# Window attention in steps of both images at once: scores and transposes share four PSUM banks

## The chip, the cores and the metric

The kernel runs on one core of one Trainium2 chip. The metric is the device time of one execution in microseconds, the median of the runs. A core has the engines TensorE (PE, matrix products and transposes), VectorE (DVE), ScalarE (ACT) and GpSimd (POOL), and SyncE (SP), which issues most DMAs. PE writes only to PSUM, eight banks of 512 float32 in each of 128 partitions; here DVE and ACT read PSUM.

## The reference, cut to what matters

The input is 16 images of 56 x 56 positions and 192 channels. Two residual layers follow each other, each behind a group norm:

```python
x = x + outlook(_gn(x), ...)          # 3 x 3 outlook attention, 6 heads
x = x + window_attention(_gn(x), ...) # 7 x 7 windows, shifted by 3, 12 heads of 16
# window_attention, per window of n = 49 positions:
attn = einsum('wmqd,wmkd->wmqk', q * hd ** (-0.5), k) + rpb + mask
attn = softmax(attn, axis=-1)
out = einsum('wmqk,wmkd->wqmd', attn, v)   # then a projection
```

## The kernel before, in words

Two images are worked on at once. Their 2 x 192 channels are laid on 3 x 128 partitions (tiles j = 0, 1, 2; tile 1 holds the end of the first image's channels and the start of the second's). A hardware loop runs over the 8 pairs of images. In an iteration comes first the outlook layer in seven chunks of eight image rows (replication products of line 481, DVE products, adds on POOL and by DMA), then the window attention in NW = 8 rows of windows.

A row holds 8 windows, that is PAIRS = 4 pairs of windows (p = 0 to 3), for two images. Before, the unit of work is a step s = 0 to 7 of a row: the pair p = s // 2 of one image m = s % 2. A step goes this way: `scores` (PE, 12 products of 32 rows x 64 columns, banks 0 to 3; the profile counts each float32 product twice), `score_bias` (DVE adds the bias to them and writes `sp_`, lines 1540 and 1543), `score_max` (DVE, 1550), `shift_step` (POOL subtracts the maximum, 1777), `exp_step` (ACT, 1127), `prob_sum` (DVE, 1557 and the reciprocal, 1560), `normalize_step` (POOL, 1784), `turn_probs` (PE, six transposes, 737, into banks 6 and 7), `keep_probs` (ACT copies them to `pt`, 1137), and for each two steps `attend` (PE, 24 products of probabilities and values into bank 7, 754) and `keep_y` (DVE, 1565). The scores run AHEAD = 3 steps ahead of the transposes. `sp_` has SOFTS = 4 buffers, `pt` has 3.

The order is written out by hand. Each engine has its own list, and semaphores that only count up join them. Into each step of PE a further piece is put by `ring(w, s)`: the projections of queries and keys of row w + 1 (`wide` makes two of the three output tiles, with two products of 64 rows and then two full ones, lines 336 to 339; `middle` makes the third, with one full product and two of 64 columns, 344 to 346), its values (`window_values`, 682 to 686), the output projection of row w - 1, transposes of the output of row w - 2 (`turn_out`, 772) and transposes of the next pair's input (`turn_next`, 375). Their results go through banks 4 and 5 (R0, R1), partly 6 and 7. ACT copies them out: `keep_queries` (1103), `keep_keys` (two ACT operations for each tile, 1110 and 1111), `keep_window_values` (1121), `keep_out` (1144), `keep_x` (971). DVE adds output and residual (`finish`, 1575, and `fin_wrap`, 1580) and takes the statistics of the next input (`stat_x`, 1285). POOL prepares the normalized input of row w + 2 (`stage_norm`, 1763) and the residual (`stage_residual`, 1770). The values are laid out block by block with DMAs (`vbd`, by `spread`).

Row 0 has a `ring_first`, and the last row a `ring_last`: there the second group norm's sums of the next pair of images (`group_means`, `deviate`, `group_variances`, `deviation` with two table loads on ACT, `coefficients`), and the start of its outlook layer (`normalize`, `logits`, `turn_logits`, softmax, `values_wide`) lie between the steps.

## Time and profile before

| | us |
|---|---|
| median of 3 runs | 3623.78 (3619.59 to 3627.0) |
| span of the profiled execution, first to last instruction | 3620.7 |
| one pair of images, from its first replication product to the next pair's | 444.6 |
| of it: outlook layer up to the first scores | 158.2 |
| of it: window attention and tail | 286.5 |

The page has no other time of the profiled execution than the span; it lies 3.1 us below the median of the runs. A pair's rows repeat almost exactly from one pair of images to the next. PE's lengths in the profile include the pipeline's end, so consecutive products overlap; how long PE is kept by a piece of work is read from its start to the start of the next.

### The profile page before, as it was taken

The page shows a single profiled execution, that of the slowest core. Times are in us where ns is not written, and L with a number is a line of the kernel's source. Part 1 is how long each engine was busy: PE and PEld are TensorE (multiplying, and loading weights), DVE is VectorE, ACT ScalarE, POOL GpSimd, SP SyncE. Part 2 cuts the span into 40 slices and gives each one's busy share as a digit, 9 for nine tenths or more (in the row PEclk, how much of TensorE's full clock was granted, in tenths as well). Part 3 has the DMA queues.
Part 4 walks back from the last instruction along what each step waited for, and adds up shares of the span by engine and source line. Part 5 has one row for each costly group of instructions (what it writes and reads, how often), then busy time and mean ns, then how long its engine had stood idle before and what let it go on. Part 6 is the DMA issues. An engine that isn't in the chain of part 4 may idle for free.

```text
span 3620.7 us, 108243 instructions
## 1 busy us (share of the span) xinstructions
PE 3391.4 (94%) x39908; PEld 1934.4 (53%) x39908; DVE 2774.4 (77%) x4977; ACT 1918.9 (53%) x4114; POOL 2401.7 (66%) x1888
## 2 busy tenths in 40 slices
PE   6999999999999999999999999999999999999999
PEld 3456654566445664456643666346663466634666
DVE  4977779677796777977779677787777877788776
ACT  3445654456545564456643656446564366644565
POOL 2867747677486774767747677577765777567775
PEclk7999999999999999999999999999999999999999
DMA  4732227322372224712246222561215512165222
GB/s 106 139 88 65 78 71 141 74 75 68 88 138 59 82 68 89 145 53 77 78 93 128 67 71 69 106 130 56 80 58 118 117 56 83 59 130 107 61 74 63
DMA packets 204359, 317.64 MB, mean 88 GB/s; under 512 B 16922, under 2 KB 176154, under 8 KB 203802
## 3 DMA queue, kind: packets, MB, share of 16 engines
q0 software_dynamic: 31936, 148.66, 21.1%
q1 hardware_dynamic: 171866, 161.61, 15.2%
q8 instruction: 343, 5.62, 0.6%
q14 instruction: 214, 1.75, 0.2%
HBM read 45.97 MB, written 38.54 MB: 23 GB/s over the span
## 4 chain that ended last, share of the span: by engine, by line
PE 65%; issue 11%; ACT 8%; DVE 8%; POOL 4%; DMA 3%; ACTq 1%; DVEq 0%; SPq 0%; POOLq 0%
PE P L737 5%; PE P L754 5%; PE P L481 5%; PE P L338 5%; PE P L336 5%; PE P L345 4%; PE P L706 4%; PE P L344 4%; PE P L682 3%; DVE prod L1435 3%; DMA prod<-prod 3%; PE P L685 2%; PE P L339 2%; ACT kbd L1110 2%; PE P L772 2%
## 5 line engine op out<-in xcount | busy, mean ns | idle before, releaser
L1777 POOL TENSOR_TENSOR sp__70<-sp__70,mx 128x588 f32<-128x588 f32 x512 | 600.1, 1172 | 603.5 <-DVE mx L1550 602.2
L1435 DVE TENSOR_TENSOR prod<-P,vpad 128x896 f32<-128x896 f32 (+1 forms) x768 | 790.3, 1049 | 131.2 <-PE P L481 118.2
L1784 POOL TENSOR_TENSOR sp__70<-sp__70,rc 128x588 f32<-128x588 f32 x512 | 600.3, 1172 | 21.5 <-DVE rc L1560 21.5
L1540 DVE TENSOR_TENSOR sp__70<-P,relb 128x196 f32<-128x196 f32 x512 | 184.2, 360 | 466.6 <-PE P L706 466.5
L1137 ACT ACTIVATE pt<-P 98x294 f32<-98x294 f32 x1024 | 429.7, 421 | 176.6 <-PE P L737 175.7
L481 PE MATMUL P<-at,sel 108*128 108x448 bf16 x1512 | 428.0, 362 | 58.2 <-DVE prod L1435 32.9
L1697 POOL DMA_DIRECT2D prod<-prod x216 | 202.0, 938 | 376.7 <-DVE prod L1435 371.7
L737 PE MATMUL P<-ident,sp__70 113*98 113x113 f32 x3072 | 390.3, 263 | 17.3 <-ACT pt L1137 10.3
L1550 DVE TENSOR_REDUCE mx<-sp__70 128x12 f32<-128x588 f32 x512 | 389.5, 761 | 9.4
L1557 DVE TENSOR_REDUCE sm<-sp__70 128x12 f32<-128x588 f32 x512 | 386.9, 756 | 10.7 <-ACT sp__70 L1127 10.5
L737 PEld LDWEIGHTS P<-ident,sp__70 113*98 113x98 f32 x3072 | 325.7, 129 | 111.6 <-issue 51.3
L1127 ACT ACTIVATE sp__70<-sp__70 128x588 f32<-128x588 f32 x512 | 360.6, 704 | 27.9 <-POOL sp__70 L1777 27.0
L481 PEld LDWEIGHTS P<-at,sel 108*128 108x128 bf16 x1512 | 113.2, 98 | 428.6 <-issue 230.6
L706 PE MATMUL P<-kbd,qs 32*64 32x98 f32 x12288 | 299.7, 260 | 17.1 <-DVE sp__70 L1543 6.6
L1713 POOL TENSOR_TENSOR psum_p<-psum_p,prod 128x1344 f32<-128x1344 f32 x96 | 301.6, 3142 | 5.7 <-DVE prod L1435 1.9
L1543 DVE TENSOR_TENSOR sp__70<-P,relb 128x392 f32<-128x392 f32 x512 | 284.0, 555 | 0.0
L706 PEld LDWEIGHTS P<-kbd,qs 32*64 32x64 f32 x12288 | 201.1, 131 | 101.0 <-issue 92.9
L1770 POOL TENSOR_SCALAR xr<-xa,bout 128x392 f32<-128x392 f32 x192 | 246.2, 1284 | 0.0
L1121 ACT ACTIVATE vs<-P 98x192 f32<-98x192 f32 x512 | 126.7, 333 | 221.4 <-PE P L682 220.6
L1046 ACT ACTIVATE xa<-P,bias 128x448 f32<-128x448 f32 x168 | 107.3, 639 | 257.0 <-PE P L499 217.9
L754 PE MATMUL P<-pt,vbd 98*32 98x49 f32 x12288 | 214.7, 213 | 28.2 <-ACT pt L1137 26.3
L1713 POOL TENSOR_TENSOR psum_p<-prod 128x1344 f32<-128x1344 f32 x56 | 171.8, 3069 | 80.7 <-DMA prod<-prod 80.7
(244 smaller groups left out, 7430.8 us busy)
## 6 DMA issues: line engine op xcount, KB each, us to landing
prod<-prod POOLq DMA_DIRECT2D x216, 672.0 KB, 5.5
vbd<-vs SPq DMA_DIRECT2D x512, 147.0 KB
xin<-in_x SPq DMA_DIRECT2D x126, 336.0 KB, 4.1
out<-ot SPq DMA_DIRECT2D x184, 168.0 KB, 2.3
out<-ot SPq DMA_DIRECT2D x80, 84.0 KB
wn<-in_L_conv_qkv_weight SPq DMA_DIRECT2D x2, 432.0 KB, 6.3
wno<-in_L_conv_proj_weight SPq DMA_DIRECT2D x2, 144.0 KB, 6.4
self<-in_sel SPq DMA_DIRECT2D x3, 91.1 KB
```

What stands on the lines that cost most here:

```text
L481: last = mm(P[:, 2 * (n % 2) + b, 0:CT], sel[:, k, :], at[:, col:col + CT], start=True, stop=True)
L706: last = mm(P[half * SLOT:(half + 1) * SLOT, r, part * 2 * N:(part + 1) * 2 * N], qs[rows, w % 2, j, tok:tok + SLOT], kbd[rows, w % 2, j, ...
L737: last = turn(P[0:2 * N, bank, c * QUERIES:(c + 1) * QUERIES], sp_[0:QUERIES, s % SOFTS, g * 2 * N:(g + 1) * 2 * N], ident[0:QUERIES, 0:QU ...
L754: last = mm(P[32 * r:32 * r + 32, Y_BANK, col:col + N], vbd[w % 2][:, 2 * p + half, m, 2 * HD * g:2 * HD * (g + 1)], pt[:, (q + m) % KEPT, ...
L1127: go(sp_[:, s % SOFTS, :], sp_[:, s % SOFTS, :], ACT.Exp).then_inc(p_exp, 1)
L1137: go(pt[:, (STEPS * w + s) % KEPT, 3 * b:3 * b + 3, :, :], src, ACT.Copy).then_inc(p_kept, 1)
L1435: tt(by_row(dst), by_row(P[:, b:b + len(op), 0:CT]), val, ALU.mult).then_inc(prod_ok, 1)
L1550: red(mx[:, b, :], sp_[:, b, :].rearrange("p (h k) -> p h k", h=NH), AX.X, ALU.max).then_inc(t_max, 1)
L1557: red(sm[:, b, :], sp_[:, b, :].rearrange("p (h k) -> p h k", h=NH), AX.X, ALU.add).then_inc(p_sum, 1)
L1713: tt(y0[:] if n == PADD - 1 else psum_p[:], slot(0) if n == 0 else psum_p[:], slot(k), ALU.add).then_inc(padd_ok, 1)
L1777: tt(per_head(sp_[:, b, :]), per_head(sp_[:, b, :]), spread(mx[:, b, :]), ALU.subtract).then_inc(t_sub, 1)
L1784: tt(per_head(sp_[:, b, :]), per_head(sp_[:, b, :]), spread(rc[:, b, :]), ALU.mult).then_inc(p_norm, 1)
```

## The change

The unit of the list becomes a pair of windows p of both images, four in a row. `scores(w, p)` issues 24 products, each four over all four row groups; the two halves m of a pair now are row groups 0 and 1 (banks 0, 1) and row groups 2 and 3 (banks 2, 3), and `COLUMN` says which tile j a row group works on. The scores run two pairs ahead. DVE adds the bias to a half in one operation of 588 columns. The twelve transposes of a pair go to the score banks 0 to 3, four to a bank, so they wait until the scores of the pair after (`t_add`) have been read, and the next scores wait until the transposes have been copied out (`p_kept`); ACT copies a half in one operation of 588. Bank 6 thereby becomes a third bank R2 for the projections. A projection is now `begin` (four narrow products, 64 columns and then 64 rows, and one full product) and `end` (two full products), with `turn_probs` or other work between; `window_values` issues its four 64-row products first and then the full ones. Each engine's list is regrouped by pairs: PE does `turn_probs`, `between`, `scores`, `attend`, `after`; ACT `early`, two copies, exp, `late`, exp. POOL does, per pair: subtract (second half), normalize (first half), a residual piece at p = 0 and 3, normalize (second half), a norm piece at p = 0 to 2 or a residual piece at p = 3, subtract (first half of the pair after). `attend` follows in the same pair rather than one step later, in another order of its 24 products. The last row is written out anew; logits go to bank 4. Number and size of all other operations and of the DMAs are as before.

Cut to its core (rows 1 to 6; of the functions of PE, ACT and DVE mostly only the added lines, shifted left):

```diff
-AHEAD = 3
-SOFTS = 4
-KEPT = 3
+AHEAD = 2
+SOFTS = 2 * AHEAD
+TURNS = NW * PAIRS
 QUERIES = SLOT + N
...
+Y_BANK, SOFT_BANK, FIRST_BANK, NEXT_BANK = 7, 7, 3, 4
 V_BANK = 4
+COLUMN = ((0, 2, 1), (1, 0, 2))
 OTOK = [min(TT, RT - TT * t) for t in range(NT)]
...
+    def begin(banks, bank, w, col, src, n):
+        a, b = P[:, banks[0], 0:n], P[:, banks[1], 0:n]
+        mm(P[LO, bank, 0:n], w[:, 0, col + 128:col + 192], src[:, 0], start=True, stop=False)
+        mm(P[HI, bank, 0:n], w[:, 2, col:col + 64], src[:, 2], start=True, stop=False)
+        mm(a, w[LO, 1, col:col + 128], src[LO, 1], start=True, stop=False)
+        mm(b, w[HI, 1, col + 64:col + 192], src[HI, 1], start=True, stop=False)
+        return mm(a, w[:, 0, col:col + 128], src[:, 0], start=False, stop=True)
+    def end(banks, bank, w, col, k, src, n):
+        b = P[:, banks[1], 0:n]
+        second = mm(b, w[:, 2, col + 64:col + 192], src[:, 2], start=False, stop=True)
+        return second, mm(P[:, bank, 0:n], mid[:, k, :], src[:, 1], start=False, stop=True)
...
+    def scores(w, p):
+        D = TURNS * i + PAIRS * w + p
+        pe.wait_ge(t_add, ONE + 2 * D)
+        pe.wait_ge(p_kept, ONE + 2 * D - 2)
...
+                for r in range(4):
+                    j = COLUMN[r // 2][n]
                     rows = slice(32 * r, 32 * r + 32)
                     tok = (2 * p + half) * N
+                    last = mm(P[half * SLOT:(half + 1) * SLOT, r, n * 2 * N:(n + 1) * 2 * N],
                               qs[rows, w % 2, j, tok:tok + SLOT],
                               kbd[rows, w % 2, j, :, tok:tok + N], start=True, stop=True)
...
+    def turn_probs(w, p):
+        D = TURNS * i + PAIRS * w + p
+        pe.wait_ge(t_add, ONE + min(2 * (PAIRS * w + p + AHEAD), 2 * TURNS) + 2 * TURNS * i)
+        pe.wait_ge(p_kept, ONE + 2 * D)
+        for m in range(2):
+            pe.wait_ge(p_norm, ONE + 2 * D + m + 1)
+            for g in range(HP):
+                last = turn(P[0:2 * N, 2 * m + g // 4, g % 4 * 2 * SLOT:g % 4 * 2 * SLOT + QUERIES],
+                            sp_[0:QUERIES, (2 * p + m) % SOFTS, g * 2 * N:(g + 1) * 2 * N],
                             ident[0:QUERIES, 0:QUERIES])
             last.then_inc(p_turned, 1)
...
         if p % 2 == 0:
             pe.wait_ge(v_in[p // 2], ONE + 64 * (R + 1))
+        pe.wait_ge(p_kept, ONE + 2 * (D + 1))
+        pe.wait_ge(y_kept, ONE + D)
+        for n in range(T):
+            for e in range(2):
                 for half in range(2):
+                    for r in range(4):
+                        if r % 2 != e:
+                            continue
+                        m = r // 2
+                        g, j = 2 * n + e, COLUMN[m][n]
+                        image = int(j == 2 or (j == 1 and m == 1))
+                        col = j * 2 * N + half * N
+                        last = mm(P[32 * r:32 * r + 32, Y_BANK, col:col + N],
+                                  vbd[w % 2][:, 2 * p + half, image, 2 * HD * g:2 * HD * (g + 1)],
+                                  pt[:, m, g, half, :], start=True, stop=True)
         last.then_inc(y_mm, 2)
...
+    def between(w, p):
...
+        elif p == 0:
             if w >= 2:
+                pe.wait_ge(y_kept, ONE + PAIRS * R)
+                turn_out(w - 2, 1, Y_BANK)
+            end_queries(w + 1)
             if w >= 2:
+                pe.wait_ge(q_kept, ONE + T * (R + 1) + 1)
+                turn_out(w - 2, 2, R0)
                 pe.wait_ge(ot_kept, ONE + NT * (R - 2) + 2)
+        elif p == 1:
+            if w >= 2:
+                pe.wait_ge(y_kept, ONE + PAIRS * R + 1)
+                turn_out(w - 2, 3, Y_BANK)
+            end_keys(w + 1)
             pe.wait_ge(k_kept, ONE + T * (R + 1) + 1)
+            turn_next(w, 0, R0)
             if w >= 2:
                 pe.wait_ge(ot_kept, ONE + NT * (R - 2) + 4)
+        elif p == 2:
+            pe.wait_ge(y_kept, ONE + PAIRS * R + 2)
+            turn_next(w, 1, Y_BANK)
+            end_out(w - 1)
             pe.wait_ge(fin_ok, ONE + T * (R - 1) + 1)
+            turn_next(w, 2, R0)
+            pe.wait_ge(x_kept, x_count + 2)
         else:
...
+    def after(w, p):
...
+        elif p == 0:
+            pe.wait_ge(q_kept, ONE + T * (R + 2))
+            if w >= 2:
+                pe.wait_ge(ot_kept, ONE + NT * (R - 2) + 3)
+            begin_keys(w + 1)
+        elif p == 1:
+            pe.wait_ge(k_kept, ONE + T * (R + 2))
             pe.wait_ge(x_kept, x_count + 1)
+            begin_out(w - 1)
+        elif p == 2:
+            pe.wait_ge(fin_ok, ONE + T * (R - 1) + 2)
+            pe.wait_ge(x_kept, x_count + 3)
+            window_values(w + 1, 0)
+        elif w < NW - 2:
+            pe.wait_ge(vs_kept, ONE + 4 * (R + 2))
+            pe.wait_ge(ot_kept, ONE + NT * (R - 1) + 1)
+            pe.wait_ge(xw_ok, ONE + T * ((NW - 1) * i + w + 2))
+            begin_queries(w + 2)
+        else:
...
     def window_row(w):
-        for s in range(STEPS):
-            turn_probs(w, s)
-            w2, s2 = ahead(w, s, AHEAD)
+        for p in range(PAIRS):
+            turn_probs(w, p)
+            if w < NW - 1:
+                between(w, p)
+            else:
+                between_last(p)
+            w2, p2 = pair_after(w, p, AHEAD)
             if w2 < NW:
-                scores(w2, s2)
-            if s % 2 == 1:
-                beside(w, s)
-            elif s > 0:
-                if w == NW - 1 and s == 6:
-                    turn_logits(CHUNKS * (i + 1), FIRST_BANK)
-                attend(w, s // 2 - 1)
-            elif w > 0:
-                attend(w - 1, PAIRS - 1)
-            if w == 0:
-                ring_first(s)
-            elif w < NW - 1:
-                ring(w, s)
+                scores(w2, p2)
+            attend(w, p)
+            if w < NW - 1:
+                after(w, p)
...
+    def keep_probs(w, p, m):
+        D = TURNS * i + PAIRS * w + p
+        act.wait_ge(p_turned, ONE + 2 * D + m + 1)
+        if m == 0:
+            act.wait_ge(y_mm, ONE + 2 * D)
+        src = P[0:2 * N, 2 * m:2 * m + 2, :].rearrange("p b (g n) -> p (b g) n", n=SLOT)[:, 0:NH, 0:N]
+        go(pt[:, m, :, :, :].rearrange("p g h n -> p (g h) n"), src, ACT.Copy).then_inc(p_kept, 1)
...
+    def early(w, p):
...
+        elif p == 0:
             keep_queries(w + 1, 0, R0)
+        elif p == 1:
             keep_keys(w + 1, 0, R0)
+        elif p == 3:
             for m in range(2):
                 keep_window_values(w + 1, 0, m, (R0, R1)[m])
...
+    def late(w, p):
...
+        elif p == 0:
+            if w >= 2:
+                keep_out(w - 2, 1, Y_BANK)
+            keep_queries(w + 1, 1, R1)
+            keep_queries(w + 1, 2, R2)
+            if w >= 2:
+                keep_out(w - 2, 2, R0)
+        elif p == 1:
+            if w >= 2:
+                keep_out(w - 2, 3, Y_BANK)
+            keep_keys(w + 1, 1, R1)
+            keep_keys(w + 1, 2, R2)
+            keep_next(w, 0, R0)
+        elif p == 2:
+            keep_next(w, 1, Y_BANK)
+            keep_next(w, 2, R0)
+        else:
             for m in range(2):
                 keep_window_values(w + 1, 1, m, (R0, R1)[m])
+            keep_out(w - 1, 0, R2)
+    def window_row(w):
+        for p in range(PAIRS):
+            early(w, p)
+            keep_probs(w, p, 0)
+            keep_probs(w, p, 1)
+            w1, p1 = pair_after(w, p, 1)
+            exp_step(w1, p1, 1)
+            late(w, p)
+            w2, p2 = pair_after(w, p, 2)
+            exp_step(w2, p2, 0)
...
+    def score_bias(w, p, m):
...
+        dve.wait_ge(p_turned, ONE + 2 * (D - AHEAD) + m + 1)
+        dve.wait_ge(sc_mm, ONE + D + 1)
+        tt(by_bank(sp_[:, b, :]), P[:, 2 * m:2 * m + 2, 0:T * 2 * N].rearrange("p r (n k) -> p r n k", n=T),
+           by_bank(relb[:, kind, :]), ALU.add).then_inc(t_add, 1)
...
+    def ahead(w, p):
+        w2, p2 = pair_after(w, p, AHEAD)
+        if w2 < NW:
+            score_bias(w2, p2, 0)
+            score_max(w2, p2, 0)
+            score_bias(w2, p2, 1)
+        keep_y(w, p)
+        if w2 < NW:
+            score_max(w2, p2, 1)
+    def window_row(w):
+        for p in range(PAIRS):
+            w1, p1 = pair_after(w, p, 1)
+            if w >= 1 and p == 3:
+                finish(w - 1, 2, R2)
+            prob_sum(w1, p1, 0)
+            if w >= 1 and p == 2:
                 finish(w - 1, 0, R0)
+            prob_sum(w1, p1, 1)
+            if w >= 2 and p == 0:
+                stat_x(i + 1, w - 2, (1, 2))
+            elif w >= 1 and p == 2:
                 finish(w - 1, 1, R1)
```

## Rows read from the trace of the kernel before

**Rows 1.** The page's first part: busy time, share, instructions.

```profile
PE 3391.4 (94%) x39908; PEld 1934.4 (53%) x39908; DVE 2774.4 (77%) x4977; ACT 1918.9 (53%) x4114; POOL 2401.7 (66%) x1888
```

**Rows 2.** Busy time by stretch, second pair of images: stretch, length, engines, granted clock, DMA.

```profile
1115.01:1121.54 6.53, 5.38 (x97) 3.82 (x97) 5.40 (x11) 3.78 (x9) 4.61 (x4) 1.00 0.01 4
1121.54:1154.85 33.31, 30.50 (x482) 20.10 (x481) 20.75 (x44) 21.39 (x54) 20.45 (x19) 1.00 0.18 55
1154.85:1186.09 31.24, 30.75 (x518) 19.79 (x519) 25.65 (x53) 18.01 (x41) 24.89 (x23) 1.00 0.17 49
1219.65:1253.20 33.55, 32.01 (x532) 20.99 (x530) 24.97 (x52) 20.17 (x49) 24.27 (x23) 1.00 0.26 77
1320.29:1354.12 33.83, 32.17 (x533) 20.85 (x530) 25.67 (x53) 20.46 (x50) 24.20 (x22) 1.00 0.18 57
1354.12:1401.47 47.35, 41.32 (x551) 27.24 (x551) 27.86 (x61) 28.63 (x60) 16.96 (x16) 0.89 0.20 60
```

**Rows 3.** PE's timeline in a generic row: start, length, line, products, idle before.

```profile
1237.98 0.82 PE L754 MATMUL P<-pt,vbd 98*32 98x49 f32 x48 [0.45 <-ACT pt L1137]
1238.73 0.59 PE L336 MATMUL P<-yt,wot 64*128 64x392 f32 x1
...
1239.59 0.93 PE L338 MATMUL P<-yt,wot 128*128 128x392 f32 x2
1240.35 0.82 PE L339 MATMUL P<-yt,wot 128*128 128x392 f32 x2
1241.01 0.75 PE L737 MATMUL P<-ident,sp__70 113*98 113x113 f32 x6
1241.69 0.58 PE L706 MATMUL P<-kbd,qs 32*64 32x98 f32 x24
1242.20 1.26 PE L375 MATMUL P<-ident,xin 112*128 112x112 f32 x8
1243.30 0.84 PE L344 MATMUL P<-yt,mid 128*128 128x392 f32 x2
1244.07 0.54 PE L345 MATMUL P<-yt,wot 128*64 128x392 f32 x1
...
1244.88 0.60 PE L375 MATMUL P<-ident,xin 112*128 112x112 f32 x4
...
1250.82 0.57 PE L682 MATMUL P<-wt,xw 128*98 128x192 f32 x2
...
1253.20 0.74 PE L737 MATMUL P<-ident,sp__70 113*98 113x113 f32 x6
```

**Rows 4.** ACT's timeline in the same stage: start, length, line, operation.

```profile
1264.76 0.68 ACT L1110 ACTIVATE kbd<-P,kb,me 128x392 f32<-128x392 f32 x1 [1.86 <-PE P L338]
...
1267.02 0.43 ACT L1137 ACTIVATE pt<-P 98x294 f32<-98x294 f32 x1
1267.32 0.71 ACT L1127 ACTIVATE sp__70<-sp__70 128x588 f32<-128x588 f32 x1
1267.90 0.43 ACT L1137 ACTIVATE pt<-P 98x294 f32<-98x294 f32 x1
```

**Rows 5.** Groups of instructions in one generic row: shapes, count, busy us, mean ns, idle.

```profile
L1777 POOL TENSOR_TENSOR sp__70<-sp__70,mx 128x588 f32<-128x588 f32 x9 | 10.6, 1172 | 10.9 <-DVE mx L1550 10.9
...
L1550 DVE TENSOR_REDUCE mx<-sp__70 128x12 f32<-128x588 f32 x8 | 6.1, 760 | 0.1
...
L1543 DVE TENSOR_TENSOR sp__70<-P,relb 128x392 f32<-128x392 f32 x8 | 4.4, 555 | 0.0
L1770 POOL TENSOR_SCALAR xr<-xa,bout 128x392 f32<-128x392 f32 x3 | 3.9, 1283 | 0.0
...
L1540 DVE TENSOR_TENSOR sp__70<-P,relb 128x196 f32<-128x196 f32 x8 | 2.9, 361 | 7.2 <-PE P L706 7.2
...
L1560 DVE RECIPROCAL rc<-sm 128x12 f32<-128x12 f32 x9 | 2.0, 228 | 0.3
...
L971 ACT ACTIVATE xa<-P 128x448 f32<-128x448 f32 x3 | 1.6, 549 | 1.6 <-PE P L375 1.5
```

743 lines of the change are left out of this document (291 added, 452 removed).

## Prediction, on record before the change was run

> **What bounds the kernel now.** The page's first lines come first: TensorE (PE) is busy 94% of the span, VectorE (DVE) 77%, GpSimd (POOL) 66%, ScalarE (ACT) 53% [rows 1]. A mean over stages says little, so next the busy time of each engine in the stretches of one image pair [rows 2]. The change touches the eight window rows and the stretches just ahead of and behind them: 6.5, 33.3, 31.2, four equal rows of 33.55 (one shown), a seventh of 33.8, then the last row with its tail, 47.35; 286.5 us of a pair's 444.6, eight times over. In the 33.55 us row PE is busy 32.0, DVE 25.0, POOL 24.3, ACT 20.2. Third, PE's timeline inside such a row, read from start to start, since a printed length includes a pipeline's end [rows 3]. It is packed: of the 1.5 us of idle time in the row 0.45 is the wait before ATTEND (L754), released by ACT's copy of the turned probabilities. So a generic row is set by PE's own work, some 32 us, and a little by ACT. Idle time on DVE and POOL costs nothing today.
>
> I write T for the 12 probability transposes of a pair of windows, S for its scores, A for ATTEND, and slot p for the PE list of pair p.
>
> **PE's work, part by part.** Before, six transposes take 1241.01 to 1241.69 = 0.68, the scores of one step 0.51 (1241.69 to 1242.20), ATTEND 0.76 (1237.98 to 1238.73) [rows 3].
> - T and S. A change of array shape costs about 0.1: behind the row halves the first full product takes 0.76 (1239.59 to 1240.35), the next 0.66. So a transpose is (0.68 - 0.1) / 6 = 0.097, and T becomes 12 x 0.097 = 1.16 when a full-shape product follows, instead of 2 x 0.68. S: a step's 12 products come as four, four, two and two, the last two at half the width of the array, so it has four places; the pair's 24 come as six times four, so six places where two steps had eight. Of the 0.51 some 0.17 is start and drain (an estimate: a shape change 0.1 and the 0.07 by which the printed 0.58 is longer). S becomes 0.34 x 6 / 4 + 0.17 = 0.68, not 1.02. Bounds: 0.60 if the start also shrinks, 1.02 if width buys nothing. I take 0.68, because ATTEND pushes the same 48 records through in 0.76.
> - On that the Trainium skill speaks against the change: "TensorE: Matmul & The Clock Gate", section "Wait — 56ns, not 53.3ns?", has a floor of about 25 ns from matmul start to start. It would make S 1.2 us in place of 0.68 and leave nothing of its gain. ATTEND's 48 records in 0.76 us, 16 ns each, say that the floor does not hold across tiles here.
> - A. Same 24 products in another order, alternating between column groups. The trace has no such order: bounds 0.5 (as much above 0.17 of start and drain as S has for the same passes) and 0.9 (0.15 more than today's); I take 0.74.
> - Projections. Before: wide half 2.28 (1238.73 to 1241.01), narrow half 0.77 + 0.81 (1243.30 to 1244.88), 3.86. After: `begin` = narrow 0.81, row halves 0.86 (1238.73 to 1239.59), one full product 0.76 = 2.42; `end` = two full products 1.32; 3.74. Three times a row, saves 0.36.
> - Window values: 2.38 (1250.82 to 1253.20) loses one shape change: 2.2, twice a row.
>
> Slots of a generic row, T + between + S + A + after: slot 0 1.16 + 2.16 + 0.68 + 0.74 + 2.42 = 7.16; slot 1 7.2; slot 2 1.16 + 2.25 + 0.68 + 0.74 + 2.2 = 7.0; slot 3 1.25 + 2.2 + 0.46 + 0.68 + 0.74 + 2.42 = 7.7. Sum 29.1 against 32.0: PE alone could give back 4.4 us a row, stalls included.
>
> **The new waits.** The transposes now lie in the score banks. So T of pair q+1 waits until DVE has read the scores of q+2, and S of q+2 waits until ACT has copied out both halves of q. That closes a loop through four engines, one turn per pair. Terms [rows 4, 5], the smaller copies at about 0.15 plus 1 ns an element, less 0.1 where the next one starts early: bias add 588 wide, from 0.36 (196) and 0.555 (392), 0.75 (bounds 0.75 and 0.92, the two parts joined); max 0.75 (the row has 0.76); POOL subtract 1.17; exp 0.59 from start to start (1267.32 to the next copy at 1267.90); two copies of 588, each from 0.43 (294) and 0.55 (448) about 0.68 long and 0.57 from start to start (bounds 0.57 and 0.73); exp of the other half 0.70; the sum as long as the max; reciprocal 0.15 of its 0.23 before the next can start; hand-offs some 0.25. Sum 6.2, plus what stands in the queues in between. On ACT ahead of the copies: one query copy 0.49, one key pair 1.13 (four halves take 2.26, 1264.76 to 1267.02), nothing, four value copies 0.84. On DVE ahead of the bias: two statistics 1.04, nothing, a finish 0.54, one 0.52. On POOL one residual (1.28) or a shorter norm stands between normalize and the subtract and adds some 0.35 in slots 1 and 3. By slots 7.7, 7.7, 6.8, 8.0: 30.2 a row, already above PE's 29.1.
>
> Now slot by slot, from T's start. Slot 0: the chain puts the bias add at 5.3 and the next T 2.28 later (bias, max, bias): 7.6; PE needs 7.16. Slot 1 is where it hurts. `begin_out` takes R0, R1 and R2, and must wait for ACT to have copied two more key tiles and an x tile, all queued behind the copies and the exp: exp of the next pair starts 0.55 after T, then 0.59, key 1.13, copies 2 x 0.57, exp 0.59, output 0.38, keys 2.26, x 0.55 = 7.2; then 2.42 of `begin_out`: next T at 9.65. PE idles about 2.4 in this slot (1.1 before S, where the output copy's wait stands behind the exp, and 1.3 here). Slot 2: all PE from there, 7.0. Slot 3: 7.7, again PE. Row: 7.6 + 9.65 + 7.0 + 7.7 = 31.95, against 33.55: 1.6 less. This is the heart of the forecast: PE gets 2.9 us cheaper, and 1.3 of it goes to waits on ACT.
>
> **The other rows of a pair.** Ahead of the first T: today 6.5 from the first scores. Now T needs both pairs' biases, and DVE, POOL and ACT do two halves of the first pair one after the other, with two key copies ahead of the second exp: about 10.2, +3.7. Row 0 has fewer PE fillers and a wait for three query copies in slot 1: 8.9 + 9.0 + 6.8 + 6.2 = 30.9 against 33.3, -2.4. Row 1 has no output work in slots 0 and 1: about 30.5 against 31.2, -0.7. Rows 2 to 5: 4 x -1.6 = -6.4. Row 6: its slot 3 has three short output turns in place of a `begin`: -2.5. Last row and tail, 47.35: the chain of group means, variances, square root and two table loads now lies ahead of the third bias add and the third exp; I get the last A about 28.4 after the row's first T, then values 4.4, output 3.75, turns and PE's wait at the loop's end, which stays: 44, with PE idle for 3.8 us ahead of the logits. PE's mean clock in this stretch is 0.89 today [rows 2], so part of it runs at 1.2 GHz; I give back 1 us for the longer idling: -2.5. No DMA is added or moved past another; the values' DMAs have 10 us from the ACT copy to their use, as now.
>
> Sum of a pair: +3.7 - 2.4 - 0.7 - 6.4 - 2.5 - 2.5 = -10.8; eight pairs -87. On the profiled span 3620.7 this is 3534; the median of the runs is 3.1 higher, 3623.8 - 87 = **3537 us**.
>
> **Rivals.**
> - *The waits on ACT are hidden* (H). If the queue order happens to fit, or copies are nearer 0.57 long, PE sets rows at 29.1 to 30.2: rows 2 to 6 give 3.5 to 4.4 each, the tail 4: 18 to 25 a pair, 3425 to 3480. For: PE's list has the fillers in every slot. Against: the 9.65 us slot is a sum of ACT's own lengths, with no free parameter.
> - *Width buys nothing* (W), the skill's floor as a mechanism of this kernel: S costs 1.02, the wide bias 0.92 and the copies 0.73. Slots 0, 2, 3 grow by 0.34, the loop by 0.5: a row of 33.0 to 33.3; 3580 to 3616. The page named above would put S at 1.2. Against: 16 ns per record in ATTEND.
> - *Slower* (C): the clock in the last row. If PE's idle time ahead of the logits drops it to 1.2 GHz and it stays there to the end of the tail, some 14 us of PE work double, +14 a pair against the 10.8 gained: 3650. It decides from 11 us per pair on. For: 0.89 today and a longer idle stretch. Against: today it comes back within the row, and the work behind is dense.
> - *No change* (N): gain and prologue cancel, 3617 to 3631.
>
> **How the numbers follow.** Forecast 0.48 (own range 3490 to 3580), H 0.18, W 0.13, C 0.15, N 0.06. No change means within 0.2%, 7 us, about what a measurement here can tell. Faster: 0.48 + 0.18 + 0.13 = 0.79; same 0.06; slower 0.15. The range for 8 in 10 takes all of the forecast's and W's cases and the nearer half of H's: 3450 to 3622.
>
> **What the new profile would show.** Generic rows of 31.4 to 32.5 us; S of 48 records in about 0.7; DVE's bias add 0.75 and ACT's copy 0.68; PE idle 1 to 1.5 us twice in slot 1, released by ACT (output copy before S, x copy before `begin_out`); DVE waiting less for scores; first T 10 us behind the first scores; the clock below 0.9 in the last row. The forecast is wrong if T itself waits for POOL's normalize in most slots (the loop is longer than 8.4 us a slot), if PE shows no idle time in slot 1, or if the stretch behind row 6 exceeds 47 us.

## The result and the profile after

The changed kernel takes **3694.0 us** (median of four runs, 3692.0 to 3694.7) against 3624.4 for the kernel before, measured beside it: ratio 1.0192, 95% interval 1.0177 to 1.0206. The forecast was 3537 with a range of 3450 to 3622. The kernel is slower, and by more than the rival that was meant to come out slower (3650).

The page's first lines of the kernel after (its span is 3692.7, that of before 3620.7), then the granted clock in 40 slices:

```profile
PE 3321.1 (90%) x39908; PEld 1964.0 (53%) x39908; DVE 2743.5 (74%) x4465; ACT 1869.8 (51%) x3602; POOL 2413.9 (65%) x1888
...
PEclk7999989999899998999989999999989999899998
```

Against [rows 1] PE is 70 us less busy, DVE 31, ACT 49. The gain in work is there, but PE is idle 142 us longer (371.6 in place of 229.3). Busy time by stretch of the fourth image pair of the kernel after, with columns as in [rows 2] (behind PE, PEld, DVE, ACT and POOL stand the granted clock and the DMA columns). First scores to first T, row 0, row 1, rows 2 to 4, the last row with its tail:

```profile
1587.90:1600.18 12.28, 10.50 (x156) 7.92 (x157) 7.94 (x13) 8.13 (x20) 7.81 (x7) 1.00 0.16 51
1600.18:1632.11 31.93, 27.36 (x504) 18.52 (x502) 20.59 (x36) 16.77 (x36) 21.57 (x21) 0.95 0.19 59
1632.11:1665.93 33.82, 30.65 (x523) 20.56 (x522) 23.25 (x41) 18.27 (x37) 24.58 (x23) 0.95 0.15 43
1665.93:1698.65 32.72, 29.74 (x531) 20.98 (x530) 24.63 (x44) 19.36 (x40) 24.45 (x23) 1.00 0.26 77
1698.65:1731.39 32.74, 29.88 (x532) 21.07 (x531) 24.65 (x44) 19.37 (x40) 24.46 (x23) 1.00 0.27 80
1731.39:1768.31 36.92, 32.51 (x531) 22.06 (x530) 24.66 (x44) 19.48 (x40) 24.39 (x23) 0.95 0.24 69
...
1833.09:1883.56 50.47, 39.00 (x466) 25.86 (x467) 27.22 (x56) 26.44 (x48) 16.15 (x16) 0.79 0.17 49
```

Read the fourth row first: at full clock a generic row takes 32.72 where the forecast had 31.95 and the kernel before has 33.55 [rows 2]. So a row at full clock gives back 0.8, half of the 1.6 forecast. Then read the clock column: before, it was 1.00 in every row but the last [rows 2]. Now it is 0.95 in rows 0, 1 and 4 of this pair and 0.79 in the last one. Over the whole span PE's clock stands at its lower level (1.2 GHz, called half clock here) for 378 us in 58 stretches. Before it was 173 us in 23, none of them in rows 0 to 6.

The same stages as medians over the eight pairs, beside the two versions of the experiments below that matter most (run 1 and run 12; a filler is a bf16 product of 512 columns whose result nobody reads, issued only to keep PE busy; the kernel before has 44 of them a pair already, all in the outlook layer):

| us per pair | before | forecast | after | run 1: after with fillers in rows 0 to 6 | run 12: best version |
|---|---|---|---|---|---|
| first scores to first T | 6.53 | 10.2 | 12.28 | 12.28 | 9.55 |
| row 0 | 33.32 | 30.9 | 32.95 | 30.85 | 31.97 |
| row 1 | 31.24 | 30.5 | 33.81 | 33.32 | 32.72 |
| rows 2 / 3 / 4 / 5 | 33.55 each | 31.95 each | 32.73 / 32.72 / 34.44 / 33.49 | 32.72 / 33.71 / 32.70 / 32.75 | 32.21 each |
| row 6 | 33.83 | 31.3 | 32.78 | 32.02 | 31.53 |
| last row and tail | 46.94 | 44.8 | 49.40 | 48.55 | 46.34 |

Slot 1 of the fourth row above on PE, the slot where the forecast had two waits:

```profile
1673.89 1.32 PE L726 MATMUL P<-ident,sp__70 113*98 113x113 f32 x12
1675.06 0.49 PE L757 MATMUL P<-ident,fin 128*112 128x128 f32 x3
1675.39 0.82 PE L656 MATMUL P<-xw,wt 128*128 128x392 f32 x2
...
1678.26 0.88 PE L713 MATMUL P<-kbd,qs 32*64 32x98 f32 x48 [1.01 <-ACT ot L1127]
1679.08 0.79 PE L749 MATMUL P<-pt,vbd 98*32 98x49 f32 x48
1680.78 0.54 PE L647 MATMUL P<-yt,wot 128*64 128x392 f32 x1 [0.91 <-ACT xa L955]
...
1682.45 0.93 PE L651 MATMUL P<-yt,wot 128*128 128x392 f32 x2
```

and on ACT, whose queue is what PE waits for:

```profile
1675.89 1.20 ACT L1120 ACTIVATE pt<-P 98x588 f32<-98x588 f32 x2
1676.97 0.70 ACT L1112 ACTIVATE sp__70<-sp__70 128x588 f32<-128x588 f32 x1
1677.55 0.48 ACT L1127 ACTIVATE ot<-P 56x384 f32<-56x384 f32 x1
1677.92 0.67 ACT L1094 ACTIVATE kbd<-P,kb,me 128x392 f32<-128x392 f32 x1
...
1679.61 0.69 ACT L1095 ACTIVATE kbd<-P,kb,me 128x392 f32<-128x392 f32 x1
1680.17 0.56 ACT L955 ACTIVATE xa<-P 128x448 f32<-128x448 f32 x1
```

T is 1.17 (1673.89 to 1675.06; forecast 1.16), S 0.82 (0.68), `begin` 2.43 (1680.78 to the next T at 1683.21; 2.42). ACT runs without a gap from T's first half to the x copy's end at 6.84 behind T's start (forecast 7.2). Both waits in slot 1 stand where they were forecast and are released by what was forecast.

### The profile page after: what moved, and what is told of

Read it like the earlier page. It is cut to its first block, busy times and chain, and to the rows that moved or that the text cites. A ratio compares the mean times of both kernels' runs of the same rounds, so it can differ in the third digit from the quotient of the medians.

```text
span 3692.7 us, 105251 instructions
## 1 busy us (share of the span) xinstructions
PE 3321.1 (90%) x39908; PEld 1964.0 (53%) x39908; DVE 2743.5 (74%) x4465; ACT 1869.8 (51%) x3602; POOL 2413.9 (65%) x1888
## 4 chain that ended last, share of the span: by engine, by line
PE 44%; POOL 16%; issue 16%; ACT 11%; DVE 8%; DMA 4%; DVEq 0%; POOLq 0%; SPq 0%; ACTq 0%
POOL sp__70 L1767 6%; POOL sp__70 L1774 4%; PE P L485 4%; DMA prod<-prod 4%; PE P L726 3%; PE P L649 3%; PE P L713 3%; DVE prod L1419 3%; POOL xr L1760 3%; PE P L647 3%; PE P L651 3%; ACT kbd L1095 2%; ACT kbd L1094 2%; DVE sp__70 L1523 2%; PE P L694 2%
## 5 line engine op out<-in xcount | busy, mean ns | idle before, releaser
L1523 DVE TENSOR_TENSOR sp__70<-P,relb 128x588 f32<-128x588 f32 x512 | 389.6, 761 | 119.8 <-PE P L713 114.1
L1120 ACT ACTIVATE pt<-P 98x588 f32<-98x588 f32 x512 | 311.7, 663 | 128.6 <-PE P L726 126.7
L726 PE MATMUL P<-ident,sp__70 113*98 113x113 f32 x3072 | 354.2, 267 | 19.5 <-DVE sp__70 L1523 19.5
L713 PE MATMUL P<-kbd,qs 32*64 32x98 f32 x12288 | 233.1, 264 | 112.0 <-ACT ot L1127 64.7
L713 PEld LDWEIGHTS P<-kbd,qs 32*64 32x64 f32 x12288 | 184.7, 134 | 170.8 <-issue 150.4
L972 ACT ACTIVATE vpad<-P,bias 128x448 f32<-128x448 f32 x171 | 108.4, 634 | 222.3 <-PE P L411 193.2
L749 PEld LDWEIGHTS P<-pt,vbd 98*32 98x32 f32 x12288 | 176.7, 114 | 56.4 <-issue 29.9
```

The lines of the kernel that those rows point to most:

```text
L713: last = mm(P[half * SLOT:(half + 1) * SLOT, r, n * 2 * N:(n + 1) * 2 * N], qs[rows, w % 2, j, tok:tok + SLOT], kbd[rows, w % 2, j, :, tok ...
L726: last = turn(P[0:2 * N, 2 * m + g // 4, g % 4 * 2 * SLOT:g % 4 * 2 * SLOT + QUERIES], sp_[0:QUERIES, (2 * p + m) % SOFTS, g * 2 * N:(g + ...
L749: last = mm(P[32 * r:32 * r + 32, Y_BANK, col:col + N], vbd[w % 2][:, 2 * p + half, image, 2 * HD * g:2 * HD * (g + 1)], pt[:, m, g, half, ...
L1523: tt(by_bank(sp_[:, b, :]), P[:, 2 * m:2 * m + 2, 0:T * 2 * N].rearrange("p r (n k) -> p r n k", n=T), by_bank(relb[:, kind, :]), ALU.add) ...
```

## Experiments

Theory to be tested: PE's waits on ACT are as forecast, and what was missed is that they let the clock fall in rows 0 to 6 too. The rival: the dips cost nothing, since PE waits anyway. "Time" is the median. The kernel before took 3622.7 to 3627.0 beside these runs. In the diffs a number on `stay_warm` is the count of fillers, then the bank.

**1. Fillers in rows 0 to 6** (two of the places shown; the others are ahead of S in slot 1 and in row 0).

```diff
                             turn_out(w - 2, 2, R0)
+                            pe.wait_ge(p_kept, ONE + 2 * PAIRS * R + 1)
+                            stay_warm(2, 0)
                             pe.wait_ge(ot_kept, ONE + NT * (R - 2) + 2)
...
                     elif p == 1:
+                        pe.wait_ge(k_kept, ONE + T * (R + 1) + 2)
+                        stay_warm(2 if w >= 2 else 4, R1)
                         pe.wait_ge(k_kept, ONE + T * (R + 2))
+                        stay_warm(1 if w >= 2 else 2, R2)
                         pe.wait_ge(x_kept, x_count + 1)
                         begin_out(w - 1)
```

> The changed kernel with short bf16 filler products (512 columns, no one reads them) in the places of rows 0 to 6 where PE waits: ahead of S, ahead of the output product of slot 1, ahead of row 0's last T. Nothing else is changed. Theory (clock): PE's waits of 0.7 to 1.8 us let the granted clock fall to half in rows 0, 1 and 2 to 6, for some 6.8 us a pair. With the fillers those rows have hardly a stretch at half clock, generic rows take 32.7 us every time, row 1 31.1, and the time is 3640 us (3630 to 3655). Rival (waits alone): PE waits for ACT in these slots whatever its clock, so the dips cost nothing and the time stays 3685 to 3697. Rival (fillers in the way): each pushes S or the output product back by part of its 0.21 us; over 3700.

Measured: **3651.7** (ratio 1.0070, 1.0047 to 1.0093), 42 us less than the changed kernel. Two rows of its fourth pair:

```profile
1616.39:1649.71 33.32, 30.84 (x530) 20.41 (x528) 23.82 (x42) 18.24 (x37) 25.60 (x24) 1.00 0.15 43
1649.71:1682.41 32.70, 31.71 (x540) 21.61 (x538) 24.62 (x44) 19.34 (x40) 24.42 (x23) 1.00 0.27 79
```

Rows 0 to 6 have no stretch at half clock left in any pair (in all 243 us in 31, the rest in the last row and ahead of the rows). The rival, that the dips cost nothing, has fallen: 42 of the 70 us come back, 5 a pair. Of these 5, 0.85 is in the last row, which got no filler, and some 0.7 a shorter standstill in rows 3 and 4 together (told of at the end). Row 1 was expected at 31.1 and takes 33.3: with row 0 ended 2.1 earlier, PE now waits 1.5 us in row 1's slot 0, a wait that row 0's slow end had hidden.

**2. Fillers in the last row too**, eight ahead of its first S and eight ahead of the logits.

```diff
                         turn_next(w, 2, R1)
+                        pe.wait_ge(p_kept, ONE + 2 * PAIRS * R + 1)
+                        stay_warm(8, 0)
                         pe.wait_ge(x_kept, x_count + 1)
...
+                        pe.wait_ge(p_kept, ONE + 2 * (PAIRS * R + 2) + 1)
+                        stay_warm(8, 0)
                         pe.wait_ge(g_std, ONE + 2 * i + 3)
                         logits(Gn, NEXT_BANK)
```

> As the run before, and eight fillers more ahead of the first S of the last row and eight ahead of its logits. Theory (clock): the two stretches at half clock in the last row (5 and 19 us behind its start, 24 us of a pair's time at 1.2 GHz) go or shrink, and the row with its tail falls from 49.4 to 45 or 46 us: 28 us less than the run before, 3612 (3600 to 3625). Rival (the last row is set by the chain of statistics, square root and table loads through DVE and ACT): under 1 us a pair, 3630 to 3655.

Measured: **3646.9** (3637.9 to 3648.5), last row 47.5. The stretch at 5 us is gone, the one at 18 us stays (82 us in all). The time lies in the rival's range: the eight and eight fillers are worth 0.6 us a pair by the medians of the runs and 1.0 by the last row of the profiled execution, not three.

**3. Half of the key copies.** From row 3 on this kernel leaves out the copy of each key tile's first half, so the scores use old keys there.

```diff
-                    go(kbd[:, w % 2, j, 0, lo:RT], P[:, bank, 0:RT - lo], ACT.Identity, bias=kb[:, j, 0:1], scale=me[:, 0:1])
+                    if w <= 2:
+                        go(kbd[:, w % 2, j, 0, lo:RT], P[:, bank, 0:RT - lo], ACT.Identity, bias=kb[:, j, 0:1], scale=me[:, 0:1])
```

> The changed kernel, but ACT makes only the second of the two copies of each key tile of windows rows 3 to 7 (the first image half of the keys is left as the rows before wrote it, so part of the scores is wrong). It takes 3 x 0.55 us off ACT's queue in slots 0 and 1 of rows 2 to 6 and touches no other engine. Theory (ACT's queue sets slot 1): slot 1 of rows 2 to 6 falls from 9.3 to 7.7 or 8.0 us, PE's 1.7 us of waits there fall under 0.4, the clock stays up in these rows: 5 rows x (1.4 + 1.1 for the clock) = 12 us a pair, 3600 us (3585 to 3625). Rival (the loop through DVE's bias add, POOL's subtract and normalize sets the slot): slot 1 stays over 9 us, 3675 to 3694.

Measured: **3596.7** (ratio 0.9923, 0.9901 to 0.9944; the profiled execution took 3614.4, the longest of five). Slot 1 goes from 9.31 to 7.77 in rows 2, 3, 5 and 6, a generic row to 31.16, at full clock without a filler (row 4 has the stall told of at the end):

```profile
1632.18:1663.34 31.16, 29.69 (x531) 20.99 (x530) 24.62 (x44) 17.64 (x37) 24.41 (x23) 1.00 0.27 81
```

PE, DVE and POOL are busy as long as before the edit, ACT 1.7 us less, and the row loses 1.6. ACT's queue sets slot 1, and nothing else does down to 7.8. The loop through the bias add and POOL does not hold it above that.

**4. Wide products first**, the old order, in `begin` and `end`, on top of the fillers.

```diff
-                    mm(P[LO, bank, 0:n], w[:, 0, col + 128:col + 192], src[:, 0], start=True, stop=False)
-                    mm(P[HI, bank, 0:n], w[:, 2, col:col + 64], src[:, 2], start=True, stop=False)
                     mm(a, w[LO, 1, col:col + 128], src[LO, 1], start=True, stop=False)
...
-                    return second, mm(P[:, bank, 0:n], mid[:, k, :], src[:, 1], start=False, stop=True)
+                    mm(P[:, bank, 0:n], mid[:, k, :], src[:, 1], start=True, stop=False)
+                    mm(P[LO, bank, 0:n], w[:, 0, col + 128:col + 192], src[:, 0], start=False, stop=True)
+                    return second, mm(P[HI, bank, 0:n], w[:, 2, col:col + 64], src[:, 2], start=False, stop=True)
```

> The changed kernel with the fillers of rows 0 to 6, and the queries', keys' and output's products in the old order: begin holds the two row halves and one full product, end the other full product, the full middle product and then the narrow pair. The same products, the same places in PE's list. Theory (what the narrow-first part of the change bought is one change of array shape, 0.1 to 0.12 us a pass, three passes a row): a generic row takes 33.0 to 33.3 instead of 32.7 us, and the time is 3665 to 3680. Rival (the order matters by where the work lies, since the third tile is finished 0.8 us later and ACT's queue is what slot 1 waits for): over 3680. Rival (nothing): 3651 as with the fillers alone.

Measured: **3658.1** (3650.7 to 3663.0), a row 32.93 in place of 32.70. So narrow-first is worth 0.23 in a generic row, net: slots 0 and 2 take 0.45 and 0.9 longer with the wide products first, slots 1 and 3 0.45 and 0.66 less, so the row's difference is not a change of array shape by itself. The whole is 6 us a run, under the 3665 to 3680 expected, and the two ranges touch (3649.1 to 3654.5 for run 1), so its sign is likely and its size open. Against it, the first scores to the first T falls to 11.83 and row 0 to 30.2.

**5. Scores and attention image by image**, on top of the fillers.

```diff
-                    for n in range(T):
-                        for half in range(2):
-                            for r in range(4):
+                    for m in range(2):
+                        for n, half, r in [(n, half, r) for n in range(T) for half in range(2) for r in (2 * m, 2 * m + 1)]:
...
-                    for n in range(T):
-                        for e in range(2):
-                            for half in range(2):
-                                for r in range(4):
-                                    if r % 2 != e:
-                                        continue
+                    for m in range(2):
+                        for g in range(HP):
+                            for half in range(2):
+                                for r in (2 * m + g % 2,):
```

> The changed kernel with the fillers of rows 0 to 6, and the 24 score products and the 24 attention products of a pair issued image by image, as before the change, so that two of the array's row places (for the scores) alternate instead of four. Banks, columns and counts stay. Theory (width buys time): S goes from 0.8 back to 1.0 or 1.1 us, A stays within 0.1 of its 0.73; four slots a row, of which two or three have no waiting to swallow it: a row 33.2 to 33.5 instead of 32.7, the time 3680 to 3705. Rival (width buys nothing): S stays at 0.8, the time 3651.

Measured: **3690.7** (ratio 1.0182), a row 33.28. In its slot 3, on PE's timeline:

```profile
1690.03 0.49 PE L754 MATMUL P<-ident,fin 128*112 128x128 f32 x3
1690.45 0.99 PE L712 MATMUL P<-kbd,qs 32*64 32x98 f32 x48
```

The attention products begin at 1691.37, so S is 0.92 from start to start, against 0.82 in the changed kernel, and they take 1.09 against 0.72. The same 96 records cost 0.47 us more in an order that goes round two of the array's four places instead of four (row groups for S, column groups for A). The expectation put the difference on S and none on A; it is the other way about. With the new layout the change's order is worth 39 us a run against this one. The kernel before had 0.76 for A [rows 3]: its order, too, was image by image and took each place twice in a row, but its layout let it go round all four, so it is the number of places that counts and not the repeat.

**6. Waits moved and split, a new order ahead of the rows.**

```diff
                         if w2 < NW:
                             scores(w2, p2)
+                        y_bank_free(w, p)
                         attend(w, p)
...
                     mm(P[HI, bank, 0:n], w[:, 2, col:col + 64], src[:, 2], start=True, stop=False)
+                    if free:
+                        pe.wait_ge(*free)
                     mm(a, w[LO, 1, col:col + 128], src[LO, 1], start=True, stop=False)
...
                 exp_step(0, 0, 0)
+                exp_step(0, 0, 1)
                 keep_keys(0, 0, R0, EDGE)
                 keep_keys(0, 1, R1, EDGE)
-                exp_step(0, 0, 1)
```

`y_bank_free` holds the waits for `ot_kept` and `x_kept` that stood ahead of `scores`; `free` is the one for `ot_kept` in `begin_keys` and for `x_kept` in `begin_out`. Not shown: `window_values(0, 1)` and its copies go to slot 0 of row 0. The fillers are fewer than in run 2, 49 a pair in place of 77, since those ahead of S in the rows are gone.

> The changed kernel with three waits moved and fillers: the wait for the bank that only the attention products write stands behind S instead of ahead of it (slots 0, 1 and 2, and slot 0 of the last row); begin_keys and begin_out wait for two of their three banks only behind their narrow products; ahead of the rows ACT takes the exp of half 1 before two key copies, and the second half of row 0's values is computed in slot 0 of row 0 instead of ahead of the first T. Theory (PE waits for ACT's queue in four places for results that it needs later): slot 0 of a generic row falls from 7.97 to 7.3 us, slot 1 from 9.3 to 8.75, the row from 32.7 to 31.5; first scores to T from 12.3 to about 10, for 1 us more in row 0; the last row 1.3 less: some 8.6 us a pair, 3575 us (3560 to 3600), faster than the kernel before. Rival (the loop through bias add, subtract, exp, normalize sets slot 0 and 3): only slot 1 and the prologue gain, 3610 to 3630.

Measured: **3596.4** (ratio 0.9920, 0.9903 to 0.9936): faster than the kernel before, 21 us more than expected. Slot 0 came to 7.75 (expected 7.3), slot 1 to 9.10 (8.75), the row to 32.23. In slot 0 the next T now waits for the second bias add, 0.27 us in this row of the best version:

```profile
1659.08 1.36 PE L728 MATMUL P<-ident,sp__70 113*98 113x113 f32 x12 [0.27 <-DVE sp__70 L1546]
```

So in slot 0 the rival is right: the loop through four engines closes there as soon as ACT's waits are out of the way. First scores to T fell by 2.7 to 9.56 and row 0 gave 1.1 of it back (30.85 to 31.96). The last row is 47.2, 0.4 under run 2, where 1.3 was expected. The whole is 50 us under run 2, with fewer fillers.

**7 and 8. The last row.** Three fillers ahead of the logits instead of eight; then none, with `normalize` moved:

```diff
                     deviation(2 * i + 2, R0)
+                    act.wait_ge(g_ready, ONE + 2 * i + 3)
+                    act.wait_ge(y_mm, ONE + STEPS * (NW * i + w))
+                    normalize(Gn, 0)
                     load_table(4 * i + 5, ACT.Exp)
                     exp_step(w, 3, 0)
                     keep_probs(w, 2, 0)
-                    act.wait_ge(g_ready, ONE + 2 * i + 3)
-                    act.wait_ge(y_mm, ONE + STEPS * (NW * i + w))
-                    normalize(Gn, 0)
```

> The version with late and split waits and fillers, but three fillers instead of eight ahead of the logits of the last row. Theory (the end of the last row hangs on the logits: from their start to the next loop's first product it was 21.0 to 23.1 us in every kernel so far, before included; and the eight fillers, at half clock 0.43 us each, end 1.6 us after ACT's last normalized tile): the logits start 1.2 to 1.6 us earlier and the row ends as much earlier, 47.2 to 45.8 a pair, 3585 us (3580 to 3590). Rival (the fillers only fill, the clock they keep is worth more): 3596 to 3605.

> As the run before, without fillers ahead of the logits, and ACT makes the three normalized tiles straight behind the square root, ahead of the second table load, an exp and a copy of probabilities. Theory (chain of group statistics, square root, normalize, logits, soft-max sets the end of the last row): the logits start 3 us earlier than in the version with eight fillers, behind a wait of under 1 us; the last row takes 44.5 us (47.2 there), the time 3575 (3565 to 3585). Rival (the last exp and the last normalize of the probabilities, 2 us later, set the last T and the tail): 3590 or more.

Measured: **3594.5** and **3594.4**, the same as in 6. The logits did start 2.3 and 2.7 us earlier (23.7 and 23.3 behind the row's start, from 26.0), but the last row takes 46.8 and 47.6 us, from 47.2. The theory as expected has fallen, and the traces say where the gain went (medians over the eight pairs):

| from the logits to the last output turn | us | of it PE idle | of it at half clock | 17.3 + half of that |
|---|---|---|---|---|
| after | 20.0 | 0.7 | 5.9 | 20.3 |
| 1 (fillers in rows 0 to 6) | 18.9 | 0.7 | 3.6 | 19.1 |
| 6 (eight fillers) | 17.7 | 0.7 | 0.8 | 17.7 |
| 7 (three) | 19.0 | 0.7 | 3.8 | 19.2 |
| 8 (normalize first) | 19.3 | 0.7 | 4.5 | 19.5 |
| 12 (below) | 18.5 | 1.0 | 1.2 | 17.9 |

In the first five kernels PE has hardly a break behind the logits, and what changes the length is how much of it runs at half clock (four of the eight pairs of run 6 have none of it and take 17.3). In runs 6 to 8 the stretch at half clock begins 14 to 18 us behind the row's start, ahead of the logits, and lasts 7 to 14 us; logits that come earlier come into it. That is not all of it, as runs 10 and 12 show in the four pairs where the logits come at 23.3 and at most 0.3 us behind them is at half clock. The stretch still takes 19.0 there, because PE waits for the copy of the probabilities and for POOL's normalize, as in the seventh pair of run 12:

```profile
3125.46 0.79 PE L751 MATMUL P<-pt,vbd 98*32 98x49 f32 x48 [1.24 <-ACT pt L1142]
...
3128.36 0.79 PE L728 MATMUL P<-ident,sp__70 113*98 113x113 f32 x6 [0.29 <-POOL sp__70 L1797]
```

The last attention product begins 30.9 us behind the row's start in these pairs as in the ones at half clock (31.1). So at full clock run 8's rival is right: the last exp and the last normalize, and not the logits, set the last attention product and with it the row's end.

**9. No fillers at all**, with the moves of 6 and 8.

> The changed kernel with the moved and split waits, the new order ahead of the rows and the normalize straight behind the square root, and no filler product at all. Theory (the clock falls where PE waits too much within a short stretch; the moved waits take 0.7 us of some 2.6 out of slots 0 and 1 of a generic row, and what is left in slot 1 stays in one piece): part of the dips in rows 0 to 6 come back, in rows 0 and 1 in most pairs: 20 to 40 us over the same with fillers, 3600 to 3615. Rival (the shorter waits are short enough): within 8 us of it, 3575 to 3585.

Measured: **3615.4** (ratio 0.9969, 0.9955 to 0.9982), 21 us over number 8, at the edge of what theory gave. Of its time 283 us are at half clock, in rows 0, 2, 3, 4 and 6 among others. The moves alone, with no filler, are worth 79 us: they turn the change from 1.9% slower to 0.3% faster.

**10 and 11. Fillers at the loop's start**, in a version of 8 with four fillers ahead of the logits, and in the kernel before.

```diff
                 pe.wait_ge(v_kept, ONE + T * (G0 + 1))
+                stay_warm(6, 0)
                 for c in range(CHUNKS):
                     outlook(c)
...
+                        pe.wait_ge(y_kept, ONE + PAIRS * R + 2)
+                        stay_warm(4, Y_BANK)
                         pe.wait_ge(g_std, ONE + 2 * i + 3)
                         logits(Gn, NEXT_BANK)
```

(the kernel before got the first part only)

> The version with the normalize straight behind the square root, with four fillers in its wait ahead of the logits (into the bank of the attention products) and six at the start of the next loop. Last time the logits came 2.7 us earlier than with eight fillers, and nothing of it reached the end of the row: from the logits to the next loop it took 24.0 instead of 21.0 us. Theory (what sets the end of the row is the last attention product, 14.5 to 15.6 us ahead of the end, and the clock under the products behind it): the last attention product stays at about 31.7, the time at half clock in the last row falls from 114 us to under 80, the one at the loop's start from 48 to under 35, and the row ends 1 us earlier: 3586 (3580 to 3592). Rival (the logits set it after all, the clock took it back): last row 45 us or less, 3575. Rival (fillers at half clock push the logits and the first product of the loop back): 3594 or more.

> The kernel before with six fillers at the start of the next loop, where PE waits 3.4 us, its only wait of over 1 us a pair that is outside the last row. Theory (the kernel before has no dips in rows 0 to 6 to win back, so fillers are worth little there): 0 to 6 us, 3618 to 3627. Rival (fillers are a gain of their own that the kernel before would have too, so that the comparison with a version that has them says little): 15 us or more, 3609 or less.

Measured: **3592.1**, and for the kernel before **3635.2** (ratio 1.0029, 1.0018 to 1.0039), which is 11 us slower with them, outside both expectations, although its time at half clock falls from 173 to 128 us. The last row and tail take 48.1 instead of 46.9 there, and 48.0 instead of 47.6 in number 10, whose last rows have 89 us at half clock in all (106 in number 8; under 80 was expected). The wait at the loop's start is not one that products can fill: it comes first, and the six products on top of it. At this place fillers are no gain for either kernel; the other places were not tried in the kernel before, whose rows have no dips.

**12. The same without the fillers of the loop's start.**

> The last version without its six fillers at the loop's start; the four in the wait ahead of the logits stay. From the traces so far: between the logits and the last output turn PE has 0.7 us of idle time in every version, and the stretch takes 17.3 us plus half of the time that it spends at half clock (after 5.9 us of it: 19.9; the version with eight fillers 0.0: 17.3; with three 3.9: 19.1; with normalize first 4.5: 19.3); then 3.7 us to the loop's first product. Theory (PE's own work behind the logits sets the end of the row, and the clock in it): logits at 23.3, 2 to 3.5 us at half clock behind them, so 18.3 to 19.0, the last row 45.4 to 46.3 instead of 47.2, and 3586 us (3580 to 3591). Rival (the fillers of the loop's start cost nothing in the last version, and something else holds the row's end): 3592 to 3597.

Measured: **3584.8** (3583.5 to 3588.4; ratio 0.9899, 0.9882 to 0.9915). The last row is 46.3, with the logits at 23.8, 18.5 us behind them and 1.2 of that at half clock. The time is as expected, but partly by luck: the sum of 17.3 and half of 1.2 gives 17.9, and the waits just told of make up the rest. Its stages, as above: first scores to T, rows 0, 1 and 3, the last row:

```profile
1544.87:1554.42 9.55, 8.13 (x141) 6.09 (x142) 7.72 (x12) 6.66 (x16) 6.87 (x7) 1.00 0.19 60
1554.42:1586.39 31.97, 30.94 (x532) 20.36 (x530) 20.25 (x36) 18.39 (x39) 21.44 (x21) 1.00 0.20 61
1586.39:1619.11 32.72, 30.04 (x526) 20.19 (x525) 23.83 (x42) 18.24 (x37) 25.60 (x24) 1.00 0.15 44
1651.33:1683.54 32.21, 31.05 (x536) 21.25 (x535) 24.51 (x44) 19.33 (x40) 24.40 (x23) 1.00 0.28 79
1779.49:1826.08 46.59, 38.89 (x476) 24.77 (x477) 27.52 (x56) 26.43 (x48) 16.08 (x16) 0.87 0.18 53
```

## Why the prediction was wrong

The forecast had a pair 10.8 us shorter. It came out 8.8 longer, a miss of 19.6 us, over eight pairs 157. Two of its steps failed. It took the clock as full in rows 0 to 6, which cost 42 us. And it priced PE's waits for ACT's copies in slot 1 of the generic rows only, and put them at nothing or too low ahead of the first T, ahead of S in slot 0, in row 1 and ahead of the first S of the last row. With the clock held (run 1, column 5 of the table) some 13.4 us a pair of the miss are left: 2.1 ahead of the first T, 2.8 in row 1, 0.8 in each of rows 2 to 6 and 1.0 more in row 3, 3.75 in the last row. So neither step alone turned the gain into a loss. The prediction's own sign of being wrong, over 47 us behind row 6, has come: 49.4. Step by step:

**The clock was placed in the last row only.** Rival C priced a fall of the clock, but only ahead of the logits. The same text put two waits of 1.1 and 1.3 us, with only S and A between them, in slot 1 of every generic row, and drew nothing from them. The windows [rows 2] show the clock at 1.00 in rows where PE is busy 32.0 of 33.55 us, so they could not say what 29.1 of 31.95 would do. Measured with run 1: 42 us, 5 a pair. With slot 1's waits taken away in run 3 the clock stays up in rows 2, 3, 5 and 6 without a filler. On this the Trainium skill's page "TensorE: Matmul & The Clock Gate", section "A second HAM failure mode: psum-queue depth-cycling", would have spoken against the change: short idle times between groups of products are enough to make the clock go up and down. This trace agrees; none of the waits in rows 2 to 6 is over 1.1 us, except the stall told of at the end.

**PE's own work: right, but for S.** T, A, `begin`, `end` and the values cost what was written (1.16, 0.72, 2.43, 1.32, 2.2). S was put at 0.68, in six places' time instead of eight, and takes 0.82: 0.13 in each slot where PE is the bound. Of the 0.20 by which it is shorter than the 1.02 of two steps before, run 5 puts half (0.92 to 0.82) on the round through all four row groups; the other half was not taken apart. The rival W (S at 1.02, rows of 33.0 to 33.3) fell, and so did, for products on different places, the floor of 25 ns from start to start that the Trainium skill's page "TensorE: Matmul & The Clock Gate" names in section "Wait — 56ns, not 53.3ns?": 48 records in 0.72 us are 15 ns each. With two places in turn they are 23 ns, near that figure.

**The waits of slot 1: right.** 9.32 for 9.65. The cause, ACT's queue, is shown by run 3. Slot 0 was 7.97 for 7.6: a wait of 0.70 ahead of its S, released by the same kind of copy as in slot 1, was priced in slot 1 and not in slot 0, where PE's 7.16 + 0.13 for S + 0.70 make the 7.97 measured. Slot 3 was 8.26 for 7.7: 0.34 of waiting for the value copies and S make most of it. Together, a generic row costs 0.8 us more than forecast, 25 us over four rows and eight pairs.

**Ahead of the first T: 12.28 for 10.2, 17 us in all.** The forecast named the two key copies that stand ahead of the second exp, and followed them through DVE and POOL. PE's own list was longer: it waits 1.2 us for those copies and 0.5 for the query copies. Run 6 took 2.7 off by exchanging ACT's order and moving the second half of the values.

**Row 1: 33.8 for 30.5.** PE waits 0.4 us ahead of S and 1.7 ahead of `begin_out` in its slot 1, and the clock falls in seven pairs of eight; where it does not, the row takes 31.14. Run 1 holds the clock and gets only 0.5 back, since PE then waits 1.5 us ahead of S in slot 0. Which engine sets that wait was not tried.

**The last row: 49.4 for 44.8.** PE's timeline of its waits in the fourth pair:

```profile
1835.83 0.98 PE L379 MATMUL P<-ident,xin 112*128 112x112 f32 x8 [0.98 <-ACT ot L1127]
1839.49 1.29 PE L713 MATMUL P<-kbd,qs 32*64 32x98 f32 x48 [2.68 <-ACT xa L955]
...
1855.59 2.49 PE L726 MATMUL P<-ident,sp__70 113*98 113x113 f32 x12 [0.19 <-DVE sp__70 L1523]
1860.44 1.00 PE L387 MATMUL P<-xn,wa_s 128*64 128x448 f32 x1 [2.36 <-ACT xn L962]
...
1868.65 0.79 PE L749 MATMUL P<-pt,vbd 98*32 98x49 f32 x48 [0.22 <-ACT pt L1120]
...
1883.56 0.92 PE L485 MATMUL P<-at,sel 108*128 108x448 bf16 x2 [3.49 <-issue]
```

The last A was put at 28.4 behind the first T and begins at 35.6 (1868.65 less 1833.09). The wait ahead of the logits is 2.4, less than the 3.8 forecast; the missing one is the 2.7 us ahead of the first S, for an x copy whose bank S does not write. Behind the last A the forecast had 16.4 and the trace has 14.9; before it was 13.0, because the wide value products (1385.49 to 1388.05) then stood ahead of the last A, and now need banks that hold the last probabilities. As C said, the clock falls in this row (0.79 in this pair) ahead of the logits, but it does not stay down to the end: it falls 5 to 8 us behind the row's start and again at 18 to 22, and is back at full speed at 29 to 33. So 5.9 us behind the logits are at half clock, and C's 14 us a pair was too much. The logits came where they were before (26.0 and 25.8 behind the row's start), and the 20.0 us behind them are 17.3 and the clock.

**The chances.** 0.79 for faster rested on H, W and the forecast all sharing one assumption, a full clock in rows 0 to 6. They were three cases of one kind and counted as three. Nor do the chances add up to the range: the forecast's 0.48, W's 0.13 and half of H's 0.18 are 0.70, not 8 in 10.

## What to carry to other kernels

Work taken off the busiest engine is worth what the waits behind it leave: price PE's idle time twice, once as time and once as clock, in every stage, and not only in the longest. Look for the same kind of wait in all slots once it is found in one. A bank's wait belongs ahead of the product that writes that bank, not ahead of the group; such moves, with two changes of order (run 9), were worth 79 us without a filler, nearly twice what fillers gave (run 1). And small products are best issued round all of the array's places (run 5).
